# Attention as diagonal blocks plus carried 32x32 states, in place of a full masked score matrix

## The reference

```python
queries = x @ q_w; keys = x @ k_w; values = x @ v_w      # 32 columns each
scores = einsum('btc,bsc->bts', queries, keys)
decay_weights = decay ** maximum(s - t - 1, 0) * (s > t)  # s: key position, t: query position
retrieved = einsum('bts,bsc->btc', scores * decay_weights, values)
attn = retrieved @ o_w.T * out_scale
```

## Time and profile before

| | |
|---|---|
| median of 3 runs | 501.11 us (500.59 to 501.36) |
| the profiled execution, its own time | 500.6 us |
| its span, first to last instruction | 498.8 us |
| granted TensorE clock | 0.997 |
| PE busy | 484.0 us, 97% |
| PEld busy | 425.3 us, 85% |
| DVE busy | 389.7 us, 78% |
| ACT busy | 224.7 us, 45% |
| POOL busy | 172.3 us, 35% |

### The profile page before, as it was taken

One profiled execution on the slowest core, in us unless ns is written; L12 is line 12 of the kernel. 1 busy time (PEld: TensorE's weight loads), 2 busy tenths in 40 slices (PEclk: granted clock), 3 DMA queues, 4 the chain that ended last, 5 costly groups with the idle time before them and its releaser, 6 DMA issues.

```text
span 498.8 us, 9722 instructions
## 1 busy us (share of the span) xinstructions
PE 484.0 (97%) x3138; PEld 425.3 (85%) x3138; DVE 389.7 (78%) x1310; ACT 224.7 (45%) x403; POOL 172.3 (35%) x307
## 2 busy tenths in 40 slices
PE   5899999999999999999999999999999999999995
PEld 3779898988989898898989989898898989889894
DVE  4696878779687887868789697878969788795875
ACT  3742717255262734616364361725526272452621
POOL 4642325344142433415243241524324243340320
PEclk9999999999999999999999999999999999999998
DMA  8300010000101001010100101010010100100000
GB/s 259 14 20 4 1 44 1 20 24 1 43 0 42 0 0 42 0 42 0 42 0 0 42 0 42 0 31 11 0 42 0 42 0 2 40 2 22 2 21 21
DMA packets 18497, 11.47 MB, mean 23 GB/s; under 512 B 944, under 2 KB 17840, under 8 KB 18480
## 3 DMA queue, kind: packets, MB, share of 16 engines
q1 hardware_dynamic: 18192, 11.25, 8.5%
q10 hardware_dynamic: 288, 0.01, 0.0%
HBM read 6.80 MB, written 4.19 MB: 22 GB/s over the span
## 4 chain that ended last, share of the span: by engine, by line
PE 94%; DVE 3%; DMA 1%; ACT 1%; issue 1%; POOLq 0%; DVEq 0%; POOL 0%
PE EX L904 23%; PE S L938 12%; PE S L940 11%; PE S L939 11%; PE ATT L997 7%; PE EX L916 6%; PE EX L924 3%; PE S L979 2%; PE S L947 2%; PE TR L865 2%; PE S L949 2%; PE S L948 2%; PE S L1016 2%; PE S L1018 2%; PE S L1017 1%; PE TR L976 1%
## 5 line engine op out<-in xcount | busy, mean ns | idle before, releaser
L938 PE MATMUL S<-xh,WH 128*128 128x512 f32 x224 | 94.1, 420 | 0.0
L940 PE MATMUL S<-xh,WL 128*128 128x512 f32 x224 | 88.3, 394 | 0.0
L939 PE MATMUL S<-xl,WH 128*128 128x512 f32 x224 | 88.3, 394 | 0.0
L904 PEld LDWEIGHTS EX<-W,hid 128*128 128x128 f32 x512 | 59.6, 191 | 1.4
L904 PE MATMUL EX<-scaled,hid 128*128 128x128 f32 x512 | 59.8, 275 | 0.0
L904 PE MATMUL EX<-W,hid 128*128 128x128 f32 x512 | 59.7, 274 | 0.0
L410 POOL TENSOR_TENSOR hidl<-hid,hidh 128x512 fp32r<-128x512 f32 x32 | 40.6, 1292 | 52.9 <-ACT hidh L511 52.9
L904 PEld LDWEIGHTS EX<-scaled,hid 128*128 128x128 f32 x512 | 58.5, 192 | 0.1
L374 POOL TENSOR_TENSOR veps_x<-mv_x,eps 128x4 f32<-128x4 f32 x16 | 3.2, 201 | 156.3 <-DVE mv_x L542 156.3
L652 DVE SCALAR_TENSOR_TENSOR OUT<-EX,coef,OUT 128x128 f32<-128x128 f32 x192 | 53.7, 342 | 1.3 <-PE EX L916 0.2
L938 PEld LDWEIGHTS S<-xh,WH 128*128 128x128 f32 x224 | 42.2, 188 | 14.7 <-DVE gate L728 4.6
(11 more groups left out here) (158 smaller groups left out, 963.5 us busy)
## 6 DMA issues: line engine op xcount, KB each, us to landing
X<-x SPq DMA_DIRECT2D x16, 256.0 KB, 2.9
out<-OUT SPq DMA_DIRECT2D x16, 256.0 KB, 2.4
W<-weights SPq DMA_DIRECT2D x1, 768.0 KB, 8.2
W<-weights SPq DMA_DIRECT2D x1, 512.0 KB, 5.8
W<-weights SPq DMA_DIRECT2D x1, 384.5 KB, 6.8
W<-weights SPq DMA_DIRECT2D x1, 384.0 KB, 6.3
mask<-falling SPq DMA_DIRECT2D x1, 256.0 KB, 11.7
W<-weights SPq DMA_DIRECT2D x1, 192.5 KB, 4.6
```

The lines of the kernel that those rows point to most:

```text
L904: ins = pe.matmul(EX[EX_BANK[e]][:, t, :], hid[e][:, j, t * P:(t + 1) * P], weight[:, j * P:(j + 1) * P], start=(e == 0 and j == 0), stop= ...
L938: pe.matmul(bank[:, :], wh, hi, start=True, stop=False)
L939: pe.matmul(bank[:, :], wh, lo, start=False, stop=False)
L940: pe.matmul(bank[:, :], wl, hi, start=False, stop=True).then_inc(unit_ready, 1)
```

## The change

The attention is cut into 128x128 blocks. Only the four diagonal blocks of the scores are still made (one unit `sc` with four fp32r products of K tile s by Q tile s). The blocks off the diagonal go through states: because the decay weight of a pair of tiles is a product of a power that depends on the key's place in its tile and one that depends on the query, a key tile's contribution to all earlier queries is a 32x32 matrix, decayed keys (kd) transposed by values. Three of these are made (unit `st`) and kept stacked in `state`, 96 rows. The queries times the powers of decay that reach each of them are `qd`, 96 rows by 384 columns.

Values stay in their own 32 columns: TH and TL have 196 columns (128 for expert 2, 4 router, 32 keys, 32 values) in place of 260, and z becomes kv. The result is made transposed, in four partition groups of 32 of ATT: four plain f32 products with 32-column weights (values by the masked diagonal block of their tile), and three more that add state^T by qd. ACT copies this [128, 128] tile to `found`, and one plain f32 product of 512 columns with `back`, a block-diagonal tile with four copies of oT, gives the four token tiles in the output space.

- On PE the ten products of L997 are gone; sc is one unit; st comes after the transposes of n1; the products for `found` stand between expert 1 and expert 2 of the group before; the product with `back` stands where L997 stood, behind f1_1.
- On ACT the kv copies are 64 wide, Q is one copy of 96 rows (`qkv` weights are laid out for it), K two copies of 32 rows; kd (128x96, times a column of powers), the copy of the states and the copy to `found` are new, the last one after a wait for PE.
- On DVE the four masked score blocks (128 to 512 columns) become one of 512 columns, and qd (96x384) is new, ahead of it.
- `UNITS` loses two entries, so each unit keeps its bank from group to group: c0 and c1 free the banks of sc and st, c2 and c3 those of a1 and b1.
- In the setup vT and vo are gone, the query/key product has 160 columns, POOL clears `back`, ACT fills it, and SP spreads `depth`, `mask` and `reach` with five DMAs in place of one.

```diff
@@ UNITS @@
-TOKW = 2 * P + E
+LOGW = P + E
+TOKW = LOGW + 2 * C
+BEHIND = NT - 1
 UNITS = ([f"tok{t}" for t in range(NT)] + ["a0", "b0", "c0", "c1", "c2", "c3"]
-         + [f"sc{t}" for t in range(NT)] + ["a1", "b1", "f1_0", "f1_1", "a2", "b2", "a3", "b3", "f2", "m0", "m1", "ut"])
+         + ["sc", "st", "a1", "b1", "f1_0", "f1_1", "a2", "b2", "a3", "b3", "f2", "m0", "m1", "ut"])
@@ SP @@
-            sp.dma_start(mask[:, :], bass.AP(diagonals.tensor, diagonals.offset + P - 1,
-                                             [diagonals.ap[0], [-1, P], [1, T]])).then_inc(mask_loaded, DMA_INC)
+            sp.dma_start(depth[:, :], bass.AP(source, start, [diagonals.ap[0], [-1, P], [1, 2]])) \
+                .then_inc(depth_loaded, DMA_INC)
+            sp.dma_start(mask[:, :], bass.AP(source, start + 1, [diagonals.ap[0], [-1, P], [1, P]])) \
+                .then_inc(mask_loaded, DMA_INC)
+            for n in range(BEHIND):
+                sp.dma_start(reach[n * C:(n + 1) * C, :], bass.AP(source, start - (P - 1) - n * P,
+                                                                  [diagonals.ap[0], [0, C], [1, BEHIND * P]])) \
+                    .then_inc(mask_loaded, DMA_INC)
@@ ACT, turn @@
-                    act.copy(z[:, t, :], tok[:, 0:P]).then_inc(z_taken, 1)
+                    act.copy(kv[:, t, :], tok[:, LOGW:TOKW]).then_inc(kv_taken, 1)
...
-                act.copy(Q[0:2 * C, :], qk_bank[0:2 * C, :])
-                act.copy(Q[2 * C:3 * C, :], qk_bank[0:C, :]).then_inc(qk_high, 1)
+                act.copy(Q[:, :], qk_bank[0:3 * C, :]).then_inc(qk_high, 1)
                 half_gate(0)
-                act.copy(K[0:2 * C, :], qk_bank[2 * C:4 * C, :]).then_inc(qk_high, 1)
+                act.copy(K[0:C, :], qk_bank[3 * C:4 * C, :])
+                act.copy(K[C:2 * C, :], qk_bank[3 * C:4 * C, :]).then_inc(qk_high, 1)
...
+                act.mul(kd[:, :, :], kv[:, 1:NT, 0:C], depth[:, 0:1]).then_inc(kd_ready, 1)
...
                 half_gate(1)
+                st, free = unit("st")
+                act.copy(state[:, :], st[0:BEHIND * C, 0:C]).then_inc(free, 1)
+                act.wait_ge(found_ready, g.count(1, 1))
+                act.copy(found[:, :], ATT[:, 0, :]).then_inc(found_taken, 1)
@@ DVE, turn @@
-                    for s in range(NT):
-                        n = (s + 1) * P
-                        sc, free = unit(f"sc{s}")
-                        dve.tensor_tensor(pr[:, s, 0:n], sc[:, 0:n], mask[:, T - n:T], ALU.mult).then_inc(free, 1)
+                    sc, free = unit("sc")
+                    dve.tensor_tensor(pr[:, :, :], sc[:, :].rearrange("p (s t) -> p s t", s=NT),
+                                      mask[:, :].unsqueeze(1).broadcast_to([P, NT, P]), ALU.mult).then_inc(free, 1)
...
+                dve.tensor_tensor(qd[:, :], qk_bank[0:BEHIND * C, 0:BEHIND * P], reach[:, :], ALU.mult) \
+                    .then_inc(qd_ready, 1)
                 masked_scores()
@@ PE, turn @@
+                bank = fill("sc")
                 for s in range(NT):
-                    if s == NT - 1:
-
-                        for t in range(NT):
-                            pe.wait_ge(c_normed, g.count(NT, t + 1))
-                            ins = pe.transpose(TR[:, t * P:(t + 1) * P], n1[:, t, :], ident[:, :])
-                        ins.then_inc(c_turned, 1)
-                    bank = fill(f"sc{s}")
-                    pe.matmul(bank[:, 0:(s + 1) * P], K[:, s * P:(s + 1) * P], Q[:, 0:(s + 1) * P],
-                              start=True, stop=True).then_inc(unit_ready, 1)
+                    here = slice(s * P, (s + 1) * P)
+                    ins = pe.matmul(bank[:, here], K[:, here], Q[:, here], start=True, stop=True)
+                ins.then_inc(unit_ready, 1)
+                for t in range(NT):
+                    pe.wait_ge(c_normed, g.count(NT, t + 1))
+                    ins = pe.transpose(TR[:, t * P:(t + 1) * P], n1[:, t, :], ident[:, :])
+                ins.then_inc(c_turned, 1)
+                pe.wait_ge(kd_ready, g.count(1, 1))
+                bank = fill("st")
+                for n in range(BEHIND):
+                    ins = pe.matmul(bank[n * C:(n + 1) * C, 0:C], kd[:, n, :], kv[:, n + 1, C:2 * C],
+                                    start=True, stop=True)
+                ins.then_inc(unit_ready, 1)
                 gates(1)
...
                     expert1(g.prev())
+                for name in ("sc", "st"):
+                    b = g.bank(name)
+                    pe.wait_ge(released[b], g.uses_before(name) + 1)
+                pe.wait_ge(qd_ready, g.count(1, 1))
+                for t in range(NT):
+                    ins = pe.matmul(ATT[t * C:(t + 1) * C, 0, :], kv[:, t, C:2 * C], pr[:, t, :],
+                                    start=True, stop=(t == NT - 1))
+                for t in range(BEHIND):
+                    ins = pe.matmul(ATT[t * C:(t + 1) * C, 0, :], state[:, :], qd[:, t * P:(t + 1) * P],
+                                    start=False, stop=True)
+                ins.then_inc(found_ready, 1)
+                if not first:
                     expert2(g.prev())
...
-                for t in range(NT):
-                    for s in range(t, NT):
-                        ins = pe.matmul(ATT[:, t, :], pr[:, s, t * P:(t + 1) * P], z[:, s, :],
-                                        start=(s == t), stop=(s == NT - 1))
-                ins.then_inc(att_ready, 1)
+                pe.wait_ge(found_taken, g.count(1, 1))
+                pe.matmul(qk_bank, found[:, :], back[:, :], start=True, stop=True).then_inc(att_ready, 1)
```

More of the change, by code:

```diff
@@ L169, in build @@
         xl = [sb(f"xl{k}", [P, T], F32R) for k in range(2)]
-        z = sb("z", [P, NT, P])
+        kv = sb("kv", [P, NT, 2 * C])
+        kd = sb("kd", [P, BEHIND, C])
+        qd = sb("qd", [BEHIND * C, BEHIND * P])
+        state = sb("state", [BEHIND * C, C])
+        found = sb("found", [NT * C, P])
         pl = sb("pl", [P, NT, P + E])
@@ L286, in build @@
         flat = [b[:, :] if len(b.shape) == 2 else b[:, :, :].rearrange("p t n -> p (t n)") for b in ALL]
-        FIRST = ["ce1", "vT", "oT", "qk", "ce", "ce_b", "vo"]
+        FIRST = ["ce1", "oT", "qkv", "ce", "ce_b"]
         MM = FIRST + ["me1", "gen", "me2", "gen_b", "ml_b", "me", "me_b"]
-        TAKEN = [name for name in MM if name not in ("ce1", "vT", "oT")]
+        TAKEN = [name for name in MM if name not in ("ce1", "oT")]
         SETUP_EX = {"me1": 1, "gen": 0, "me2": 1, "gen_b": 0, "ml_b": 0, "me": 1, "me_b": 1}
@@ L364, in _ @@
             const(pool.memset(ident[:, :], 0.0))
+            const(pool.memset(back[:, :], 0.0))
             const(pool.affine_select(out=ident[:, :], in_=ident[:, :], compare_op=ALU.not_equal, fill=1.0, base=0,
@@ L498, in turn @@
                             high_weights(n)
+                        act.wait_ge(setup_act, ACT_SETUP)
+                        for t in range(NT):
+                            act.copy(back[t * C:(t + 1) * C, t * P:(t + 1) * P], oT[:, :]).then_inc(back_laid, 1)
                         act.wait_ge(w_loaded[LOAD_OF["sw_w2"]], DMA_INC)
@@ L705, in turn @@
                 for t in range(NT):
-                    dve.wait_ge(z_taken, g.count(NT, t + 1))
-                    dve.tensor_tensor(pl[:, t, :], S[g.bank(f"tok{t}")][:, P:TOKW], tokb[:, :], ALU.add) \
+                    dve.wait_ge(kv_taken, g.count(NT, t + 1))
+                    dve.tensor_tensor(pl[:, t, :], S[g.bank(f"tok{t}")][:, 0:LOGW], tokb[:, :], ALU.add) \
                         .then_inc(released[g.bank(f"tok{t}")], 1)
@@ L891, in fold_last @@
                 ins.then_inc(setup_mm, 1)
-            after("vo")
+            after("ce_b")
             def project(g, e, unit, weight):
@@ L1046 @@
 DECAY_STEPS = 10
-POOL_CONSTS = 12
-ACT_SETUP = 6
+POOL_CONSTS = 13
+ACT_SETUP = 5
 def kernel(**inputs):
```

67 lines of the change are left out of this document (38 added, 29 removed).

## The result

The changed kernel takes 489.2 us (median of 4 runs, 488.32 to 489.64), the kernel before beside it 501.24 (4 runs, 500.59 to 502.0): ratio 0.9755, interval 0.9741 to 0.9769. The forecast was 504.6 with a range of 495.8 to 515.8, so direction and size were wrong. The likeliest case (A) did not come; C, the faster side, did, and went further than its own price.

What follows compares the result with a forecast made beforehand. PE, 97% busy and 94% of the chain, was taken to bound the kernel. Terms summed to +0.22 us per group, times 16 +3.5, from 500.6 to 504.1, with the median 0.5 above: 504.6 us, range 495.8 to 515.8.

Steps and rivals of the forecast that it cites:

- A: Products for `found` on PE: strips overlap, two trips at 0.33 us; 504.6 us, own range 500.5 to 509; chance 0.40.
- C: Small PE products: trips 0.22 us each, state passes 0.16, total 1.55; -0.20 per group, 497.9 us; chance 0.29.
- scores: Four 128-column score products on PE take 0.54 us for 0.83, including 0.10 kept for K low: -0.29 per group.
- `found`, 14 passes: Seven products for `found` on PE, overlapping across strips: +0.95 us per group, between 0.86 and 1.50.
- st, 6 passes: Three state products on PE, 60 ns a pass: +0.36 us per group, between 0.16 and 0.67.
- two trips: Weight shape changes on PE around st and `found`, 0.33 us each: +0.66 per group (0.44 to 0.88).
- first half: From `ut` to the scores, DVE with PE: shorter copies bring work earlier, -0.10 us per group (0 to -0.20).
- pass b of a product runs beside pass a of the next, and 14 passes need 8 slots: Products for `found`: one product's two passes share a strip, neighbouring products overlap; 0.86 us, taken as 0.95.
- B: Products at four partition groups run one after another: 14 passes 1.50 us, +0.86 per group, 514.9 us; chance 0.26.
- the forecast's sign at four places per group: PEld idle with no releaser at four places per group would show the forecast right; no size given.
- The break-even: Scores, sum, `back` and first half give 1.75 us per group, which the small products may cost; forecast 1.97.
- D: Token products on PE: 196-column fp32r products lose speed, 0.16 us apart; with A 512.9 us; chance 0.05.

Runs made afterwards that it cites:

- one-strip experiment: Changed kernel with all seven products for `found` writing one partition group (output not the attention's): 505.73 us, ratio 1.0093 to the kernel before.
- doubled states: Changed kernel with the three state products issued twice into the same bank, six more passes: 490.64 us, ratio 0.9787 to the kernel before.
- 260 columns: Changed kernel with token products widened again by 64 columns of zeros: 489.51 us, ratio 0.9765 to the kernel before.
- Q in two copies: Changed kernel with ACT's high half of Q copied in two pieces again, 64 and 32 rows: 492.54 us, ratio 0.9824 to the kernel before.
- tile by tile: Changed kernel with each tile's state product right behind its value product in `found`: 489.68 us, ratio 0.978 to the kernel before.
- one more trip: Changed kernel with expert 2 between value and state products, so 32-column weights are entered and left once more: 495.36 us, ratio 0.9889 to the kernel before.
- One trip for both: Changed kernel with ACT's first-turn setup work put later, plus st moved behind expert 1, right before `found`'s products: 486.74 us, ratio 0.9707 to the kernel before.

## Why the prediction was wrong

By its own steps, per steady group, forecast against chain:

| step | forecast | measured |
|---|---|---|
| attention sum gone | -2.23 | -2.23 |
| scores | -0.29 | -0.41 |
| `back` | +0.87 | +0.86 |
| `found`, 14 passes | +0.95 | +0.43 |
| st, 6 passes | +0.36 | +0.07 |
| two trips | +0.66 | +0.68 |
| first half | -0.10 | -0.20 |
| sum | +0.22 | -0.80 |

Of the difference of 1.02, 0.81 is in the small products, 0.12 in the scores, 0.10 in the first half, and -0.01 in the others. (`found` is 0.36 + 0.21 less the 0.14 of entering; st is 0.19 and 0.02 of the transposes, less 0.14.) The forecast's own bounds did not reach this far: with every cost of A at its low end it had -0.39 per group, 495. Those bounds (-0.39 to +0.68, 495 to 512) don't agree either with the range that it gives A, 500.5 to 509.

**The step that failed** is "pass b of a product runs beside pass a of the next, and 14 passes need 8 slots", with its tenth for issue: `found` was put at 0.95 and cost 0.43. It took the strips for lanes that are entered in the order of the program. They act as queues of their own. A block then costs what its busiest strip has to stream, here four passes of 0.107 = 0.43. The one-strip experiment shows the other end: 1.65 less 0.14 is 1.51, the 1.50 of the forecast's B within 0.01, and 3.5 times the 0.43. The Trainium skill (TensorEngine Tiling (Array Packing), Tiling Modes, Key Properties) says that different tiles can load weights and multiply in parallel, and the trace agrees, with the 7 ns between strips. The other page weighed in the forecast (the Trainium skill, TensorE: Matmul & The Clock Gate, Part 3, Measured speedup vs the span model) gives 2.38x for three column tiles, by which the forecast had an estimated 0.63; the measurement for four is 0.43.

**The same fault in st.** 60 ns a pass was taken as the price of issuing one. The earlier trace rows has the closest spacing of any passes in the kernel before, and that is 107 ns, with 128-column weights. I let this row stand for issue in general, when what it shows is one kind of load. The doubled states give 11 ns a pass. The low end that the forecast wrote down (0.16, columns alone) was above the truth too, as it counted the three strips one after another.

**What was right.** `back` (0.86 for 0.87). The trips: 0.33 each was a choice between 0.22 and 0.44, from the setup at half pace, where 0.14 and 0.30 were read; at full pace they are 0.14 and 0.20, so the entering did not shrink and the leaving did. The sum came out right by a value between two bounds, without this being foreseen, and that is in part luck. The PEld idle with no releaser, the forecast's sign at four places per group, shows at two: 0.17 ahead of st and 0.20 behind `found`. Ahead of `found` it is 0.12, too short for the view to print, and behind st the loads go on without a gap, though the product after them pays its 0.20. The break-even was right as well: with the other terms as forecast, the small products may cost 1.75. They cost 1.18 (0.43 + 0.07 + 0.68), and it is this sentence that the decision should have hung on, since a serial run of everything (2.61) was far above it and a parallel one far below; the 1.97 in between needed strips that half overlap, and nothing in the trace spoke for just that.

**The rivals.** C came (faster, from 1.75 us down), for half of its reasons: the state passes are even shorter than it said (0.07 for 0.16), but the trips did not fall to 0.22. What carried the gain is an overlap that C took over from A unexamined. B is refuted here by the chain, and its price confirmed by the one-strip kernel. D is out: the token passes of 196 columns take 0.11, as all the others.

**Scores.** Four times 128 columns cost 0.42, which is 0.105 each with nothing over; it lies within the ends of the forecast (0.34 to 0.66). The 0.10 that the forecast kept for the wait for K low is not there: the four products' first load begins 0.06 after DVE's K low ends (226.20 + 0.69 = 226.89, and 226.95), and PE gets to them at 227.19, 0.30 after K low.

```profile
226.95 0.52 PEld L1004 LDWEIGHTS S<-Q,K 96*128 96x128 f32 x4 [0.20 <-DVE K L770]
```

**First half.** The chain gives -0.20: the first nine token passes 0.11 for 0.12 (-0.09), the fourth token product 0.36 for 0.29 (+0.07), c2 and c3 0.28 and 0.25 for 0.37 and 0.32 (-0.16), the two passes behind the fourth -0.02. So the stall for the u moments takes back most of what the narrower token products won, which the forecast had said, and the gates' silu comes earlier. In the kernel before, Q low waited for ACT's second copy; now it starts when DVE is free:

```profile
223.65 0.38 DVE L747 BATCH_NORM_AGGREGATE mv_c<-stats_c 128x2 f32<-128x6 f32 x4
224.06 0.69 DVE L767 TENSOR_TENSOR Q<-ATT,Q 32x512 fp32r<-32x512 f32 x1
```

Undone in the changed kernel, the widths give back 0.05 and the copy 0.11 ahead of the scores, 0.16 of the 0.20. Yet the same copy, put into the kernel before together with K's two copies, brings 0.02. Of the 0.25 that its loss costs in the changed kernel, 0.13 is the second wait at the scores, and that one does not show in the kernel before. What else there (kv copies of 213 ns for the 267 of z, the moved banks, K in two copies) makes up the rest was not separated.

**The covers held.** Nothing waits before `found`, `back` or st in the steady group; ACT's new wait for `found` (2.1 us of it each turn) has nothing behind it that PE needs sooner. The moved states show that the cover of `found` was real: with gates(1) and expert 1 taken out from between, 0.34 us of waiting appears.

**What was not seen at all** is the first turn. The forecast priced the start by POOL's clear and SP's DMAs, and left out what ACT has in front of the gelus there; +1.27 where it had -0.5 to +1. Of the 33.69 us of this turn 1.8 came with the clock of the profiled execution; without it, at 31.92, the turn is 0.50 shorter than before, 0.3 short of the group's own -0.80. With ACT's order put right and the setup's pace 0.8 us later it is 30.56, 1.9 less than before, so what could be had there is more than what the new order of banks took away. This cost belongs to the order of work on ACT and not to the attention.

## What to carry to other kernels

Products with 32 output partitions written to four partition groups run side by side: price such a block by the passes of its busiest strip and add one trip (0.34 us at full pace) for each time the weights go from wide to narrow and back, and do not count on merging two trips where the second block has to wait for what the first one made (0.34 saved and 0.34 waited here). When an unknown cost lies between a serial and a parallel price and the break-even between them, the forecast is a choice between the two; a value in the middle needs a mechanism of its own. When a list of rotating buffers changes its length, check the first turn by itself, where setup work stands in front of the releases, and compare it in several executions: the clock moved this one by 1.8 us.

## What the runs showed of the hardware

- Each strip works off its own products, whatever the order they are issued in: with those of one strip next to each other (L1026 and L1029 in turn) the block takes 0.59 us, with them apart 0.57. First passes of different strips start 7 ns apart, and 13 ns apart with a product of another strip issued between them. Passes start out of the order of the program across strips.
- A plain f32 pass with 32-column weights and 32 columns costs 11 ns when three strips share the work (0.07 for six); within one strip such passes start 31 to 33 ns apart.
- Entering 32-column weights costs 0.14 us and leaving them 0.20, at 2.4 GHz; in the setup, at half that pace, 0.14 and 0.30.
- After 1.6 to 1.7 us in which PE did nothing the granted clock was 0.55, then 0.50 in the changed kernel, and 512 columns took 0.43 us; it was back at 30 us. So it is in four profiled executions (the changed kernel, the state products twice, 260 columns, Q in two copies; first turns of 33.69 to 33.87 us); in three others (one strip, tile by tile, one more trip) it stayed at 1.00 after the same wait. The four had come to the pace of 2.4 GHz in the setup 5.6 to 6.1 us after the first token product, the three 3.5 to 4.6 us after it. "One trip for both" came to it late too (5.9 us), had no such wait, and stayed at 1.00. What decides was not tested.
- In the setup the recorded granted clock does not tell the pace: 260-column passes are 0.21 to 0.22 us apart at a recorded 1.00 in the kernel before (14.6 to 17.4 us), 196-column passes 0.21 at 0.50 in the changed kernel (14.4 to 17.1 us). In a steady group they take 0.12 and 0.11 at 1.00.
